# A scan layer on one Trainium2 core: two state sums stand sooner in TensorE's program, and a second product of step input and B is split by states between VectorE and GpSimd

## The reference

```python
xz = (xn @ fc1_w.T + fc1_b) @ in_proj_w.T
xc, z = split(xz, 2)                      # 512 channels each
u = silu(conv4(xc) + conv_b)
dt_low, Bm, Cm = split(u @ x_proj_w.T, [16, 32])
dt = softplus(dt_low @ dt_proj_w.T + dt_proj_b)
A = -exp(A_log)                           # 512 channels x 16 states
# for each step t:
hstate = exp(dt_t[..., None] * A) * hstate + (dt_t * u_t)[..., None] * B_t
y_t = einsum('bdn,bn->bd', hstate, C_t)
y = (y + u * D) * silu(z)
s = (y @ out_proj_w.T) @ fc2_w.T + fc2_b
g = silu((silu(xn @ wg.T) * (xn @ wu.T)) @ wd.T)
x = x + s * silu(g)                       # as the reference nests them
```

## Time and profile before

| | |
|---|---|
| median of 3 runs | 2783.31 us |
| lowest and highest run | 2783.25 and 2787.44 us |
| the profiled execution | 2788.2 us, of it span 2786.4 us |
| busy, share of the span: PE, DVE, ACT, POOL | 91%, 84%, 72%, 72% |
| mean granted TensorE clock | 0.966 |
| scan layer | from about 860 us to the end |

### The profile page before, as it was taken

How to read it: one execution, slowest core, us unless ns; L and a number is a source line. 1 busy time by engine, 2 the same in 40 slices (tenths; PEclk the granted TensorE clock), 3 DMA queues, 4 the chain that set the end, 5 groups by cost and what they waited for, 6 DMA issues and landing times. The chain is left out here.

```text
span 2786.4 us, 37406 instructions
## 1 busy us (share of the span) xinstructions
PE 2542.0 (91%) x13454; PEld 1490.8 (54%) x13454; DVE 2333.8 (84%) x2899; ACT 2011.2 (72%) x3253; POOL 2013.2 (72%) x682
## 2 busy tenths in 40 slices
PE   7897899999976799999999999999999999999988
PEld 3454344443443465656656566565655656556565
DVE  7685777777733899898998989989899898998996
ACT  4222466666643798897988979889798897988974
POOL 0656011111211999999999999999999999999996
PEclk9898999999978799999999999999999999999999
DMA  6337999888541231321313213132131321313210
GB/s 188 116 116 179 260 218 236 205 200 224 211 161 49 105 130 29 117 92 46 130 26 119 92 46 130 25 120 92 46 130 24 121 92 46 130 24 114 92 46 8
DMA packets 121586, 316.00 MB, mean 113 GB/s; under 512 B 15517, under 2 KB 76445, under 8 KB 104878
## 3 DMA queue, kind: packets, MB, share of 16 engines
q1 hardware_dynamic: 91210, 233.32, 27.3%
q0 software_dynamic: 27888, 79.24, 10.3%
q10 hardware_dynamic: 2304, 1.05, 0.2%
HBM read 278.89 MB, written 43.13 MB: 116 GB/s over the span
## 5 line engine op out<-in xcount | busy, mean ns | idle before, releaser
L1523 DVE TENSOR_TENSOR_SCAN l_st<-l_p_a,l_hl,l_st 128x512 f32<-128x512 f32 x768 | 930.2, 1263 | 90.5 <-ACT l_p_a L1808 83.3
L1721 POOL TENSOR_TENSOR l_st<-l_st,lw_cs 128x2048 f32<-128x2048 f32 x192 | 878.4, 4634 | 3.2 <-ACT l_hl L1813 3.2
L1808 ACT ACTIVATE l_p_a<-l_dt,lw_a_neg 128x512 f32<-128x512 f32 x1024 | 666.5, 681 | 67.2 <-DVE keep_xg L1523 41.1
L1713 POOL TENSOR_TENSOR l_st<-l_bs,l_dtu 128x2048 f32<-128x2048 f32 (+1 forms) x128 | 555.1, 4337 | 57.2 <-PE l_p_y L2098 53.3
L2098 PEld LDWEIGHTS l_p_y<-keep_ident,l_st 128*128 128x128 f32 x3072 | 355.1, 145 | 118.6 <-issue 73.0
L2098 PE MATMUL l_p_y<-keep_ident,l_st 128*128 128x128 f32 x3072 | 380.5, 281 | 28.7 <-POOL l_st L1721 28.7
L1020 ACT ACTIVATE a_pr<-a_p_s 128x512 f32<-128x512 f32 x512 | 284.7, 596 | 143.8 <-PE a_p_s L1089 140.0
L931 DVE TENSOR_REDUCE a_mpart<-a_p_m 128x1 f32<-128x512 f32 x512 | 312.0, 679 | 12.2 <-PE a_p_m L1045 11.0
L1523 DVE TENSOR_TENSOR_SCAN keep_xg<-l_p_a,l_hl,keep_xg 128x512 f32<-128x512 f32 x256 | 314.5, 1265 | 1.6
L1721 POOL TENSOR_TENSOR keep_xg<-keep_xg,lw_cs 128x2048 f32<-128x2048 f32 x64 | 299.7, 4682 | 2.0 <-ACT l_hl L1813 2.0
L858 POOL DMA_DIRECT2D a_w<-in_w_dram x32 | 23.1, 737 | 327.2 <-PE a_p_m L1119 271.3
(11 more groups left out here) (246 smaller groups left out, 4007.9 us busy)
## 6 DMA issues: line engine op xcount, KB each, us to landing
l_bs<-s_bc SPq DMA_DIRECT2D x64, 1024.0 KB, 4.7
lw_cs<-s_bc SPq DMA_DIRECT2D x64, 1024.0 KB, 4.7
a_w<-in_w_dram POOLq DMA_DIRECT2D x32, 1024.0 KB, 12.0
late<-in_w_dram POOLq DMA_DIRECT2D x32, 1024.0 KB, 19.4
kx<-s_kp SPq DMA_DIRECT2D x96, 256.0 KB, 12.3
s_kp<-late SPq DMA_DIRECT2D x96, 128.0 KB, 2.1
s_vp<-late SPq DMA_DIRECT2D x16, 544.0 KB, 3.5
a_vg<-s_vp SPq DMA_DIRECT2D x16, 544.0 KB, 14.8
```

The lines of the kernel that those rows point to most:

```text
L1523: eng.tensor_tensor_scan(st[k % NG][:, n, :], p_a[:, n, :], st[k % NG][:, n, :], hl[:, k, n:n + 1], ALU.mult, ALU.add).then_inc(scan_ok, 1)
L1713: eng.tensor_tensor(st[n][:, first:NG, :], bs[:, 4 * n + first:4 * n + 4, :], dtu[(k // NG) % 2][:, :].unsqueeze(1).broadcast_to([P, NG - ...
L1721: eng.tensor_tensor(st[n][:, :, :], st[n][:, :, :], cs[:, 4 * n:4 * n + 4, :], ALU.mult).then_inc(cm_ok, 1)
L1808: eng.activation(p_a[:, n, :], dt[c % 2][:, :], ACT.Exp, scale=a_neg[:, c, m:m + 1]).then_inc(dA_ok, 1)
```

## The change

Three edits. In TensorE's program `step_low(2)` and `sums(1)` stand ahead of `mix(0)` instead of behind it (with the row of `FILLS` that belongs to it), and `sums(9)` stands ahead of `gate_h(2)` and `up_h(1)`. Slot 5 is split like slot 9: GpSimd makes states 2 and 3, VectorE states 0 and 1, after the second `mixed`.

```diff
-                 ("op", 0, END, 0), ("dt", 2, SCAN, 1), ("op", 1, END, 1), ("cv", 0, FRONT, 0), ("z", 0, SCAN, 1),
+                 ("dt", 2, SCAN, 1), ("op", 0, END, 0), ("op", 1, END, 1), ("cv", 0, FRONT, 0), ("z", 0, SCAN, 1),
...
-        DRIVE_V, HALVED = (0, 2, 4, 6, 8, 9, 10, 12, 14), (9,)
+        DRIVE_V, HALVED = (0, 2, 4, 5, 6, 8, 9, 10, 12, 14), (5, 9)
...
                         last_residual(1)
                     if scan:
+                        dbu(s, 5)
                         scan_unit(s, 4, 3)
...
                     if scan:
                         sums(s, 0)
+                        step_low(q, s, 2)
+                        sums(s, 1)
                     if end:
                         mix(q, f, p, 0)
                     if scan:
-                        step_low(q, s, 2)
-                        sums(s, 1)
                         sums(s, 2)
                     if end:
                         mix(q, f, p, 1)
...
                     if scan:
+                        sums(s, 9)
                         gate_h(q, s, o, 2)
                         up_h(q, s, o, 1)
-                        sums(s, 9)
```

## The result

The changed kernel takes **2803.94 us** (median of 4 runs, 2801.5 to 2814.86), the one before 2784.86 beside it (2783.25 to 2787.44): a ratio of 1.0075, 95% interval 1.0047 to 1.0103 (the two medians alone give 1.0069). It is slower by 19.1 us. The forecast was 2797, the range ended at 2803: the direction was right, the size was not, and the median lies 0.9 us outside. The profiled execution of the changed kernel is its longest, 2814.86 us with a span of 2813.0; against the 2786.4 of before that is 26.6 us, so more than a quarter of what the two traces differ by is not in the medians.

The account below looks back on a forecast made before the run. A closed ring of waits through TensorE, ScalarE and VectorE, without GpSimd, was taken to bound the kernel. Delay of hidden(1) 11.4, gate_z(1) 1.3 and q = 16 1.1 gave 2783.3 + 13.8 = 2797 us; range 2780 to 2803.

Parts of the forecast that it names:

- The ring: Closed waits: TensorE up_h(5) to gate_z(1), ScalarE, VectorE slots 6 to 12, ScalarE, gate_z(2), ScalarE, VectorE to hidden(4); 116.215 us.
- Nothing gained by relieving GpSimd: Slot 5's halved product takes 2.19 us a tile off GpSimd, which has at least 0.22 to spare: no gain.
- rival 1: At TensorE's wait before sums(13): GpSimd's waits bind after all, so the kernel gets faster, 2769 or 2752; chance 0.13.
- the estimate of 2752: Busiest-engine rule applied to GpSimd: 2.2 us off each of 14 tiles, 31 us in all.
- `hidden(1)` later by 0.69 or 0.91: On VectorE, waiting for up_h(1) behind the moved sums(9): 0.69 us in six tiles, 0.91 in eight, 11.4 in all.
- my lower bound of 0.59: Least delay of hidden(1), from another row of sums taking 1.74 us; 0.81 in tiles with a fall of the clock.
- The signs: Period 116.9 to 117.2, stated waits at hidden(1), up_h(5) and slot 6; GpSimd's 2.00 and 1.44, ScalarE's 3.54 gone.
- The leak of 0.1 a tile: VectorE's half product delays ScalarE's gate_z(0) by 0.81, so TensorE's gate_z(1) by 0.1 us; 1.3 in all.
- the bound of 0.25: Upper bound, in us a tile, on the delay of TensorE's gate_z(1) caused by VectorE's half product.
- The tail of 1.1: In q = 16 VectorE's half product shifts scan (4,3), gate_z(0) and the scans from slot 6: +1.1 us.
- the clock's term: Falls of the granted clock on TensorE; the forecast sum added no time for them.
- Rival 3: Clock falls more often or between up_h(5) and gate_z(1): 14 x 1.1 = 15 us more, 2812; chance 0.07.

Follow-up runs that it names:

- the last kernel: Kernel before with sums(9) moved, hidden(1) later, hidden(3) to hidden(5), ScalarE's logarithm steps and VectorE's step size sooner: 2773.62 us, ratio 0.9947.
- the three early `hidden`: Kernel before with only hidden(3), hidden(4) and hidden(5) one step sooner in VectorE's program: 2794.48 us, ratio 1.0028.
- the later `hidden(1)`: Changed kernel with hidden(1) behind scan (12,0) in VectorE's program instead of ahead of it: 2803.15 us, ratio 1.0059 to the kernel before.
- the doubled product: Changed kernel with TensorE writing the step-size product of step_low(0) twice into its bank: 2812.16 us, ratio 1.0096 to the kernel before.
- the kernel with the early logarithm: Kernel before with sums(9) moved, hidden(1) later, hidden(3) to hidden(5) sooner, ScalarE's logarithm steps ahead of one exponential and state column: 2784.83 us, ratio 0.9991.

## Why the prediction was right and wrong

**The ring: right in the main.** TensorE from `up_h(5)` to `gate_z(1)`, VectorE's `hidden(4)` before it. Delaying it by the moved sum alone makes the period 0.55 longer and brings a ratio of 1.0074 (the whole change has 1.0075); shortening it, in the last kernel, is a gain. One link was missing: behind `up_h(5)` the ring passes `down(0)`, whose bank hangs on ScalarE's logarithm. No wait of the trace of before showed that.

**Nothing gained by relieving GpSimd: right. That it is clear of the ring: only just.** The half product alone, which takes 2.2 us a tile from GpSimd, gives 1.0013 [1.0004, 1.0021], slower. That decides against rival 1, and against the estimate of 2752 by the rule of the busiest engine (the Trainium skill, "Perfetto Trace Analysis", Identifying the Most-Contended Engine). But GpSimd's wait before slot 13 stands close behind VectorE's. The kernel before with the three early `hidden` alone waits 1.44 us for GpSimd and takes 116.65; with the ninth sum moved and `hidden(1)` later besides, that wait is gone and the period is 116.26. So the moved sum, which loses time by itself, may well be needed for the gain of the last kernel; that kernel without it wasn't tried.

**`hidden(1)` later by 0.69 or 0.91: right in place, too large.** Measured 0.55 a tile with the moved sum alone, just under my lower bound of 0.59. The moved row takes 1.80 up to the next instead of 1.84 (2400.54 to 2402.34 above), and `gate_h(2)` up to `up_h(1)` 1.72 instead of 1.82: 0.14 less, which is all that 0.55 is short of 0.69. I had priced the move as a whole row added; the rows behind it moved closer too. The 0.91, meant for tiles with a drop 10 us behind the statistics row, has no counterpart: 13 x 0.55 = 7.2 us where I had 11.4.

**The signs.** The places were right, several sizes not. `hidden(1)` waits 0.46, not 0.7 to 0.9. TensorE's wait for VectorE before `up_h(5)`, forecast at 1.5 to 2 us, is 0.68, with 0.45 before `step_low(1)`. Before slot 6, 0.88 is left, not 0.7. Of GpSimd's 2.00 before slot 5, 0.46 is left; its 1.44 is gone. The period of the tiles without a drop, 116.94, is at the lower edge of 116.9 to 117.2 and that of the others beyond it. ScalarE's 3.54 is gone, and GpSimd waits 2.32 for TensorE before the half product of slot 9.

**The leak of 0.1 a tile: right in place, too small.** 0.18, inside the bound of 0.25; 13 x 0.18 = 2.3 us. With the half product alone ScalarE's `gate_z(0)` begins 1.03 us behind the start of `sums(3)` instead of 0.20, so 0.83 later (0.81 was forecast), and TensorE's `gate_z(1)` 1.86 behind it instead of 1.74. The other 0.06 wasn't found.

**The tail of 1.1: too small.** +4.5 in the profiled execution. The half product alone has 2.0 and the early second sum alone 1.8; I had costed the latter at nothing, by the full tiles, and had not asked what its wait meets in a period where GpSimd is late. The rest is open: the kernel with the ninth sum alone also has 323.5, with a drop of some 1.7 in it.

**The step that failed is the clock's term: the sum had it at nothing.** Rival 3 gave a worse place of the clock's drops a chance of 0.07 and 1.1 us each. It happened, in every second tile, and costs 1.69: 118.62 or 118.63 against 116.94. Six of them are 10.1 us, the largest single term of the trace. The price was wrong because I took it from TensorE's busy time (111.3 against 110.2), in tiles where part of a drop lies over TensorE's waits; in the ring's stretch the two rows are 0.85 and 0.88 longer. The chance was too low because I gave no reason why the drops should stay where they were. The sum over the tiles is 7.2 + 2.3 + 10.1 = 19.6 of the 20.3 us measured; the other 0.7 is the first tile, 117.68, with its two drops elsewhere. This is the account of the traced execution, the slowest of four; the other three weren't traced, so how many drops they had isn't known. That the forecast came within 7 us of the median is luck in part: one error went up (11.4 for 7.2), two went down (0 for 10.1, 1.1 for 4.5).

**What is shown of the drops, and what isn't.** In the four kernels whose TensorE waits 0.21, 0.45 and 0.68 us within 6 us before `up_h(5)` (the change, the ninth sum alone, the later `hidden(1)`, the doubled product) most drops behind the first tile lie there; in the ten others, the kernel before among them, none does. There the drops in the tiles lie some 10 us behind the statistics row, where TensorE has another wait of 1.06, and cost the period nothing but in the one kernel named above. That the waits draw the drops is the reading that these fit; that their length or number decides it wasn't tried. The kernel before waits 1.19 and 0.22 at the same place and has no drop there; the kernel without the moved sum (1.41, and none before `up_h(5)`) has none either.

Why one of several alike tiles has a drop and the next has none, the traces do show: the drops keep a step of their own, and a tile has one only when that step brings it to one of the places. Before, they come 116.05 us apart and the tiles 116.22, so a drop's place slides from 10.6 us behind the statistics row to 9.4, and then there are none. In the kernel with the early logarithm the tiles take 116.04, and all of the last 14 have a drop, at 10.3 to 10.5. In the changed kernel two tiles take 235.57 and the drops come 235.52 apart, so every second tile has one. In all fourteen traces those at the first place begin 9.4 to 10.6 us behind the row and those in the ring's stretch 65.2 to 66.0. The kernel without the moved sum has its drops in the first four tiles and again in the last four, sliding by 0.34 a tile, so its drops had their turn at every place, and none lies in the ring's stretch. So the number of drops in one trace hangs on the period too, and says little by itself: that the doubled product has eight and the change six shows nothing about how full TensorE is.

## What to carry to other kernels

Price a move by the closed ring of waits, not by the engine with the highest share: here one sum of 1.8 us put ahead of a row that VectorE waits for cost 0.74%, while the same sum with short steps on ScalarE and VectorE re-ordered around it, which left every engine as busy as it was, gained 0.5%. After each wait that is removed, look for the one that takes its place and for what that one waits for: here the period went from 116.77 with the ninth sum alone to 116.26, 116.04 and 115.23, and only the last of these is faster than before beyond doubt. And when small waits of TensorE gather in the stretch that bounds the period, look in the trace whether the clock's drops have come there too: here each then cost 1.69 us.

## What the hardware did that I had not expected

A drop of the granted clock to half for 3.4 us costs a tile nothing where TensorE has waits behind it to make up for it (116.2 in tiles of before with and without one). This wait of TensorE stands in the kernel before in a tile without a drop; in the tile from 1073 to 1189 us, which has one, it is not there:

```profile
2137.73 1.96 PE L2114 MATMUL l_p_w<-l_xnT,lw_g_int 128*128 128x512 f32 x4 [0.80 <-ACT l_hT L1884]
```

In the ring's stretch a drop costs 1.68 us (118.45 against 116.77 with the ninth sum alone). Which of the two places it takes changed together with waits of 0.45 and 0.68 us. The drops have a step of their own, 116.05 us where the tiles took 116.22 or 116.04, so a period 0.2 us longer or shorter changes how many tiles have one. And a wait on TensorE can cost more than the idle time shown in front of the row: 0.58 us in brackets, 0.81 in the period.
